# The one-hot of the source remainder, stored chunk by chunk in a graph kernel

## The reference

```python
# attention layer: 12 heads of 64
e = leaky_relu(a1[src] + a2[dst]);  ee = exp(e - segment_max(e, dst)[dst])
alpha = ee / segment_sum(ee, dst)[dst]
agg = segment_sum(alpha[:, :, None] * ft[src], dst)
# relational layer, three times
msg = einsum('nd,rde->rne', h, w_rel)[edge_type, src] * inv[dst, edge_type][:, None]
h = relu(segment_sum(msg, dst) + h @ w_root + bias)
```

## Time and profile before

| | |
|---|---|
| time, median of three runs | 2808.84 us (2806.64 to 2812.04) |
| span of the profiled execution | 2808.8 us |
| PE busy | 2302.6 us (82%) |
| DVE busy | 1309.6 us (47%) |
| L415, matmuls of the windows | 1032, 255.7 us |
| L304, comparisons for `oh_key` | 516, 255.0 us |
| L257, comparisons for `oh_rem` | 20, 22.3 us |

### The profile page before, as it was taken

How to read it: one execution, slowest core, us unless ns; L and a number is a source line. 1 busy time by engine, 2 the same in 40 slices (tenths; PEclk the granted TensorE clock), 3 DMA queues, 4 the chain that set the end, 5 groups by cost and what they waited for, 6 DMA issues and landing times.

```text
span 2808.8 us, 36704 instructions
## 1 busy us (share of the span) xinstructions
PE 2302.6 (82%) x13674; PEld 2042.3 (73%) x13675; DVE 1309.6 (47%) x1838; ACT 525.6 (19%) x994; POOL 251.4 (9%) x137
## 2 busy tenths in 40 slices
PE   3988860002788887999999999999999999999996
PEld 3988860000333336899898999999999999999996
DVE  7876744799999995421211214311212133121233
ACT  0122220001455553110101102200101022010100
POOL 0011210043110000000000000010000000101000
PEclk9999885555999998999999999999999999999998
DMA  0133333101101003221221201221212111313131
GB/s 15 44 76 80 86 83 114 67 28 54 37 36 52 37 18 99 69 73 54 61 59 39 74 12 41 69 68 37 80 46 64 37 35 60 84 42 83 54 95 60
DMA packets 103671, 162.98 MB, mean 58 GB/s; under 512 B 68847, under 2 KB 68950, under 8 KB 103511
## 3 DMA queue, kind: packets, MB, share of 16 engines
q1 hardware_dynamic: 66000, 100.11, 11.8%
q0 software_dynamic: 37520, 60.59, 8.0%
HBM read 129.53 MB, written 30.66 MB: 57 GB/s over the span
## 4 chain that ended last, share of the span: by engine, by line
PE 56%; DMA 2%; DVE 2%; issue 1%; ACT 0%; DVEq 0%; SPq 0%
PE pp L976 30%; PE pa L946 26%; DMA back<-s_x 1%; DMA out_dram<-back 1%; DVE norm_stats L1073 0%; PE pp L956 0%; DVE acc L1069 0%; DMA w_raw<-in_L_gnn_w_root_dram 0%; DVE g_lo L1156 0%; DVE back L1085 0%; DVE w_lo L1145 0%; DVE acc L1121 0%; DVE back L1069 0%; DVE h_lo L1104 0%; DVE h_lo L1108 0%
## 5 line engine op out<-in xcount | busy, mean ns | idle before, releaser
L946 PE MATMUL pa<-ct_in,h_hi 125*128 125x250 f32 x2850 | 705.4, 287 | 34.0 <-issue 34.0
L946 PE MATMUL pa<-ct_in,h_lo 125*128 125x250 f32 x2850 | 702.8, 285 | 0.0
L1156 DVE TENSOR_TENSOR g_lo<-pa,g_hi 128x250 fp32r<-128x250 f32 x400 | 166.7, 417 | 1110.0 <-ACT g_hi L1050 1109.7
L946 PEld LDWEIGHTS pa<-ct_in,h_hi 125*128 125x128 f32 x2850 | 556.5, 195 | 43.5 <-issue 42.3
L946 PEld LDWEIGHTS pa<-ct_in,h_lo 125*128 125x128 f32 x2850 | 558.9, 196 | 0.9
L976 PE MATMUL pp<-w_hi,g_hi 128*125 128x384 f32 (+2 forms) x1600 | 434.8, 353 | 8.6 <-DVE g_lo L1156 8.5
L976 PE MATMUL pp<-w_lo,g_hi 128*125 128x384 f32 (+2 forms) x1600 | 430.2, 350 | 0.0
L1050 ACT CAST g_hi<-pa 128x250 fp32r<-128x250 f32 x400 | 147.1, 368 | 1437.4 <-PE pa L946 1437.4
L976 PE MATMUL pp<-w_hi,g_lo 128*125 128x384 f32 (+1 forms) x1520 | 405.4, 348 | 0.0
L796 PE MATMUL po<-pw,xh 125*65 125x418 f32 x720 | 283.3, 533 | 79.1 <-DVE pw L733 78.3
L976 PEld LDWEIGHTS pp<-w_lo,g_hi 128*125 128x125 f32 (+1 forms) x1600 | 294.6, 187 | 11.1
(11 more groups left out here) (154 smaller groups left out, 1209.8 us busy)
## 6 DMA issues: line engine op xcount, KB each, us to landing
ct_in<-s_ct POOLq DMA_DIRECT2D x45, 1220.7 KB, 16.8
s_ct<-ct_stage SPq DMA_DIRECT2D x30, 610.4 KB
w_raw<-in_L_gnn_w_rel_dram SPq DMA_DIRECT2D x39, 384.0 KB, 3.1
uv<-s_uv SPq DMA_DIRECT2D x24, 610.4 KB
w_raw<-in_L_gnn_w_rel_dram SPq DMA_DIRECT2D x21, 448.0 KB, 3.3
uv<-s_scores SPq DMA_DIRECT2D x12, 610.4 KB
w_raw<-in_L_gnn_w_root_dram SPq DMA_DIRECT2D x13, 384.0 KB, 3.1
x_tile<-in_x_dram SPq DMA_DIRECT2D x10, 375.0 KB
```

Source lines behind the costliest of these rows:

```text
L946: ins = nc.tensor.matmul(pa[0:rows, n % 2, 0:GP], a, b, start=i == 0, stop=i == len(pairs) - 1)
L1156: nc.vector.tensor_tensor(g_lo[0:rows, n % 3], pa[0:rows, n % 2, 0:GP], g_hi[0:rows, n % 3].bitcast(F32), ALU.subtract).then_inc(lo_done, 1)
```

## The change

`oh_rem` gets the shape `[CH, NCH, LANES]` with `LANES` = 128: all columns of a chunk lie side by side, and two columns of zeros follow the column of ones. VectorE makes it with one comparison per chunk, 320 of 125 elements, in which the chunk's remainders are read as one scalar per partition from `edge_cols`; `rem_16` and its cast go. `iota_rem` becomes one row of 125 16-bit numbers. GpSimd fills the ones and the zeros with two instructions. The weights of L415 and `zero_a` have 128 columns in place of 126, and so has `win`; the copy out of PSUM still takes 126 rows.

```diff
-        iota_rem = sb("iota_rem", [CH, T, REM_B], FP16)
-        rem16 = sb("rem_16", [CH, NCH], FP16)
+        iota_rem = sb("iota_rem", [CH, T], U16)
...
-        oh_rem = sb("oh_rem", [CH, T + 1, NCH], BF16)
-        zero = sb("zero_a", [CH, T + 1], BF16)
+        oh_rem = sb("oh_rem", [CH, NCH, LANES], BF16)
+        zero = sb("zero_a", [CH, LANES], BF16)
...
-        win = ps("win", [T + 1, 2, 2, 512], F32)
+        win = ps("win", [LANES, 2, 2, 512], F32)
...
-            nc.gpsimd.iota(iota_rem[:], [[1, T], [0, REM_B]], channel_multiplier=0, **counted).then_inc(consts, 1)
+            nc.gpsimd.iota(iota_rem[:], [[1, T]], channel_multiplier=0, **counted).then_inc(consts, 1)
...
-            nc.gpsimd.memset(oh_rem[:, T], 1.0).then_inc(consts, 1)
+            nc.gpsimd.memset(oh_rem[:, :, T + 1:LANES], 0.0).then_inc(consts, 1)
+            nc.gpsimd.memset(oh_rem[:, :, T:T + 1], 1.0).then_inc(consts, 1)
...
-            nc.vector.tensor_copy(rem16[:], tp[0:CH, 0, 0:NCH]).then_inc(edges_ready, 1)
-            dve.wait_ge(edges_ready, 3)
-            dve.wait_ge(consts, 9)
-
-            for i in range(0, NCH, REM_B):
-                nc.vector.tensor_tensor(oh_rem[:, 0:T, i:i + REM_B], iota_rem[:],
-                                        rem16[:, None, i:i + REM_B].to_broadcast([CH, T, REM_B]),
+            dve.wait_ge(edges_ready, 2)
+            dve.wait_ge(consts, 10)
+
+            for i in range(NCH):
+                nc.vector.tensor_scalar(oh_rem[:, i, 0:T], iota_rem[:], edge[:, 0, i:i + 1], None,
                                         ALU.is_equal).then_inc(rem_ready, 1)
...
-                            win[:, w % 2, m, 0:BANK * KEY].rearrange("p (s r d) -> p r s d", s=BANK, r=R)
+                            win[0:T + 1, w % 2, m, 0:BANK * KEY].rearrange("p (s r d) -> p r s d", s=BANK, r=R)
...
-            pe.wait_ge(rem_ready, NCH // REM_B)
-            pe.wait_ge(consts, 9)
+            pe.wait_ge(rem_ready, NCH)
+            pe.wait_ge(consts, 10)
...
-                            ins = nc.tensor.matmul(win[:, p, m, 0:BANK * KEY], oh_rem[:, :, bass.ds(q * CG + b, 1)].rearrange("e s c -> e (s c)"),
+                            ins = nc.tensor.matmul(win[:, p, m, 0:BANK * KEY], oh_rem[:, bass.ds(q * CG + b, 1), :].rearrange("e c s -> e (c s)"),
```

More of the change, by code:

```diff
@@ L28 @@
 CG = 4
-REM_B = 16
+LANES = 128
 NRUN = NCH // CG
@@ L318, in _ @@
         def _(act):
-            act.wait_ge(consts, 9)
+            act.wait_ge(consts, 10)
             def keep_turned(g):
```

## The result

The changed kernel takes 2813.3 us (median of 17 runs, 2811.0 to 2818.3), the kernel before 2807.6 us (17 runs beside them, 2806.3 to 2813.1). The ratio is 1.0018, 95% interval 1.0011 to 1.0026: slower by some 5.7 us, which is small but outside the noise. 2818 was forecast, so the time is 5 us off. The experiments show that two terms of the sum missed by more than that, in opposite directions.

A forecast was written before the change was run, and what follows sets the result against it. The prediction took the count stage to set the whole time, with a bare VectorE build, then TensorE's weight load with VectorE close behind. 2808.8 + 30.5 (build) - 21 (stream) = 2818 us, range 2803 to 2831.

The forecast's parts named there:

- The build, +30.5: VectorE's one-hot build at the start: 320 small comparisons replace 20 large ones, adding 30.5 us, range 27 to 41.
- The load, 140 ns or less: TensorE's weight load in the windows: falls from 308 ns to near 140 ns or less.
- the pitch of 0.169: Time from one window matmul to the next if the load hides: 0.169 us instead of 0.217.
- The stream, -21 us: Window matmuls after the start: shorter weight load saves 21 us, range 15 to 27, limited by VectorE's comparisons.
- Every microsecond by which the count stage ends earlier moves the run by one: Count stage's end: any shift there passes one for one into the whole time; later stages are untouched.
- two of its own signs: Signs of being wrong: the stage shrinks by less than 15 or more than 27 us; time after it changes.
- the forecast's own case: Whole kernel: slower, at 2814.4 to 2824 us, chance 0.50.
- between: Whole kernel within 0.2%: comparison pitch of 0.14 to 0.15, or stream gain of 25 and more; chance 0.20.
- Pointer free: Build: scalar pointer costs nothing, pitch 0.103, build 33 us, total 2798 us; chance 0.12, shared with TensorE gain far above 21.
- Rate lost: Build: odd length 125 loses the 2-byte rate, pitch 0.20, total time 2829 us; chance 0.12.
- Load not shorter: Window weight load does not get shorter, so only the build counts: total time 2839 us; chance 0.06.
- Of the clock: TensorE's idle time could widen low-clock stretches; each further 3 us takes back some 1.5 us; no chance of its own.

The follow-up runs named there:

- e7: Changed kernel plus three extra series of 160 comparisons ahead of the build: 0.103 us each with immediate scalar, 0.195 with 4-byte elements, 0.163 with 124 elements; no kernel time given.
- e1: Kernel before with 128 weight columns, old gapped layout and old build kept: 2789.4 us, ratio to before 0.9933.
- e2: Changed kernel with 126 weight columns side by side, without the two zero columns: 2814.65 us, ratio to before 1.0026.
- e3: Changed kernel with each 125-row store of counts cut into 112 and 13 rows: 2793.9 us, ratio to before 0.9955.
- e4: Kernel before with 128 weight columns in the old gapped layout and stores cut into 112 and 13 rows: 2765.9 us, ratio to before 0.9857.
- e5: Kernel before with 128 gapped weight columns and stores cut at 115 rows, not 112: 2783.2 us, ratio to before 0.9915.
- e8: Kernel before with only its stores cut into 112 and 13 rows: 2793.2 us, ratio to before 0.9954.
- e9: Changed kernel with five of the eight window matmuls of each run, counts wrong: windows take 320.35 us, 4.9 less than in the changed kernel.
- e10: Kernel before with five of the eight window matmuls of each run, counts wrong: windows take 333.7 us, 21.5 less than in the kernel before.

## Why the prediction was right, and where it was not

**The build, +30.5: right.** +29.0 at the first window matmul. The pitch was reckoned at 0.167 and is 0.163. Its two steps were each off, and cancel: a comparison lasts 0.283 us in after where 0.243 was said, and the next one starts 0.120 before its end, not 0.075. In e7 the same comparison lasts 0.253 at the same pitch, so the duration is no measure of the price. The parts of the pitch hold one by one in e7: 0.103 without the pointer, where 0.07 + 0.033 was said; 0.195 at the 4-byte rate, where 0.20 was said; 0.060 for the pointer, where two pointers of 0.06 were read from L304's pitch. The Trainium skill's formula in "VectorE: DVE Perf Modes", errata section, from which the prediction had an estimate of 93 ns, is near the 103 of the immediate form and far from the 163 of this one; the measurement decides.

**The load, 140 ns or less: right** (98), and the pitch of 0.169 came out as 0.162. That the columns alone could bring the gain was left open, and e1 shows that they can; e2 shows the same of the neighbourhood.

**The stream, -21 us: mis-sized, it is -30.0** and outside the range of 15 to 27 that was given. The sum of the term holds; its inputs were too cautious in one place above all. The nine windows that hold GpSimd's additions were set at a loss of 0.25 each, 2.3 in all, because TensorE waits there for VectorE and stands at the low clock. From their first `zero_a` matmul to the closing one they take 83.2 us before and 78.2 after: a gain of 5.0. The waits for VectorE are there as forecast, but ahead of them the slots come free sooner, and behind them the last matmuls are quicker, as the two timelines above show for one of the nine (8.49 to 7.91 us). That is 7.3 of the nine us, though the stretches just ahead of these windows grow by 2.1, so a part of it has only moved.

All else in the stage gains 24.9 us, where 23.3 was forecast: the 41 other windows gain 31.6 and the stretches between windows lose 6.7 (65.6 before, 72.3 after). The first window, with 12 runs, takes 21.23 us instead of 23.79. In the second, with six, a run takes 9.36 / 6 = 1.56 us instead of 10.77 / 6 = 1.80; the forecast had 1.64 for it, with 0.09 for a loop step that does not show. The late windows with two runs mostly take 2.81 to 2.89 from the first matmul to the closing one, instead of the forecast 2.99. The five that follow the additions and start at the low clock take 3.53 to 4.14, one of them longer than in before (4.14 against 3.56), and some of the next ones 2.98 to 3.17.

VectorE's waits for TensorE went from 58.3 to 47.1 us, down by 19% and not by a third or more.

**"Every microsecond by which the count stage ends earlier moves the run by one": this step failed.** The prediction read, in its first paragraph, that the stage after the windows depends only on their end. In fact it also depends on the stores, and the rows for it stood in its own table: in the earlier trace rows the DMA share of a late tile is 0.37 and 0.38, at 91 and 83 GB/s, in a stretch where TensorE is always at work and in one where it waits. With the windows' start 29 us later and their end where it was, ten tiles of stores must leave in 325 us instead of 355, and over the last tiles SyncE's queue has no slack left. By the timeline the tail grows from 35.3 to 40.7. e3, e4, e5 and e8 show the cause by spreading and not spreading the stores over more engines. e9 and e10 agree: with shorter windows than in after and in before, their tails are longer, 43.7 against 40.7 and 38.2 against 35.3. Without this loss the measured terms, +29.0 - 30.0, would give -1.0 on 2808.8, no change. The measured slowdown comes from a term that the prediction had put at 0.

**The sum: the number is luck in part.** By the profiled executions the gain of the stream was 9.0 us larger than forecast and the build cost 1.5 less; against that stand 5.4 us of tail and 1.8 behind it that were put at 0. So 10.5 us of error one way meet 7.2 the other way. "Slower" came out, but not for the reason given: build and stream, which were to make it, cancel. By two of its own signs the prediction was wrong: the stage shrank by more than 27 us, and the time after the stage changed. 2813.3 lies in the range of 2803 to 2831, just outside the bounds of the forecast's own case (2814.4 to 2824) and on the edge of the case called "between" (within 0.2%, a chance of 0.20). The reason given for that case, that matmuls also end sooner and slots come free sooner, is what after shows.

**The rivals.** Pointer free: refuted by e7. Rate lost: refuted by e7. Load not shorter: refuted, 98 ns. Of the clock: 58.0 us at the low clock in the windows before and after, so no effect there. None of them was the one that acted: SyncE's queue, off the critical path up to the last window, holds what comes after it.

## What to carry to other kernels

Separate a layout change from what rides on it: two zero columns in the old layout gave the gain (18 us) without the build that turned it into a loss. Before putting "unchanged" behind a stage that becomes shorter, add up what the DMA queues must move in it and read their share: a flat share well below one, with stores that have no gap between them, was a bound here, and the number of rows per DMA set it. With 125 rows, the cut at 112 took 14 to 24 us off three kernels here (before, after and e1).

## What the hardware showed that was not expected

- A weight load's time depends on the distance between the columns: 126 columns of 2 bytes take 308 ns at 640 bytes apart and 136 side by side, 128 columns 173 and 98. At 173 ns it no longer delays a stream of matmuls of 375 columns; at 308 it does, by 0.055 us each (pitches 0.217 and 0.162, at the high clock).
- With the load hidden the matmul is also shorter by the profile: a median of 323 to 326 ns in all three layouts, where the kernel before has 380.
- Stores of 125 rows run at 82 to 88 GB/s while only they are in the queue; cut into 112 and 13 rows they run at 200.
- The queue is held for the difference: 9.3 us for the last tile's stores with the cut at 112, 23.7 without, and attention's first load, which stands behind them, is issued at 415.1 and not at 432.6.
